# Pair 1 made as eight block products, its banks and its statistics order changed, in a graph-convolution kernel

## What is computed

```
h = relu(layernorm(x))                       # over the 1024 nodes
sim = cosine similarity of the nodes' mean;  adj = sim + gumbel0 > 1 - sim + gumbel1
nmask = adj or adj.T or eye;  common = nmask @ nmask.T
W = adj * common * common / max(common);     Wn = dinv * W * dinv
out = x + einsum(Wn, einsum(h, weight)) + bias
```

## Time and profile before

| | us |
|---|---|
| median of 3 runs | 839.84 (839.77 to 840.04) |
| the profiled execution | 838.23 |
| its span, first to last instruction | 836.5 |
| PE busy | 808.0 (97%) |
| DVE, ACT, POOL busy | 579.1, 495.9, 301.3 |

### The profile page before, as it was taken

How to read it: one execution, slowest core, us unless ns; L and a number is a source line. 1 busy time by engine, 2 the same in 40 slices (tenths; PEclk the granted TensorE clock), 3 DMA queues, 4 the chain that set the end, 5 groups by cost and what they waited for, 6 DMA issues and landing times.

```text
span 836.5 us, 13491 instructions
## 1 busy us (share of the span) xinstructions
PE 808.0 (97%) x4718; PEld 425.0 (51%) x4718; DVE 579.1 (69%) x689; ACT 495.9 (59%) x515; POOL 301.3 (36%) x255
## 2 busy tenths in 40 slices
PE   4999999999799999999999999999999999999997
PEld 3445466754345554555455545554555455545553
DVE  7999998699866656665666566656665666566652
ACT  3888826598466656665666456646655666456631
POOL 4788710300333334333433343334333333333320
PEclk9999999999999999999999999999999999999999
DMA  8999923001932222322232222222222222233111
GB/s 342 409 409 346 421 110 128 25 1 50 344 109 101 101 101 101 100 100 100 100 100 100 100 100 100 100 100 100 100 100 100 100 100 103 102 121 101 51 51 75
DMA packets 30121, 113.14 MB, mean 135 GB/s; under 512 B 3472, under 2 KB 3600, under 8 KB 29072
## 3 DMA queue, kind: packets, MB, share of 16 engines
q1 hardware_dynamic: 30096, 112.80, 36.8%
HBM read 79.23 MB, written 33.55 MB: 135 GB/s over the span
## 4 chain that ended last, share of the span: by engine, by line
PE 81%; DVE 13%; issue 3%; DMA 1%; ACT 1%; POOL 0%; DVEq 0%; SPq 0%; POOLq 0%; ACTq 0%
PE ps L891 65%; PE ps L808 8%; DVE stats L1001 8%; PE ps L907 2%; PE ps L743 2%; PE ps L826 2%; DVE moments L1007 1%; DMA out_dram<-obuf 1%; DVE ybuf L1022 1%; DVE a L1181 1%; DVE obuf L1263 0%; DVE a L1112 0%; PE ps L761 0%; PE ps L754 0%; DVE hring L1029 0%
## 5 line engine op out<-in xcount | busy, mean ns | idle before, releaser
L891 PE MATMUL ps<-a,ybuf 128*128 128x512 f16 x2604 | 571.0, 379 | 6.5 <-DVE ybuf L1105 3.4
L891 PEld LDWEIGHTS ps<-a,ybuf 128*128 128x128 f16 x2604 | 252.3, 98 | 302.7 <-DVE ybuf L1105 3.6
L1105 DVE TENSOR_TENSOR ybuf<-zbuf,ybuf 128x1024 f16<-128x1024 f32 x124 | 164.9, 1330 | 154.2 <-ACT ybuf L514 154.2
L389 POOL TENSOR_TENSOR zbuf<-zbuf 128x512 f32<-128x512 f32 x31 | 39.4, 1271 | 434.7 <-ACT zbuf L495 434.7
L514 ACT ACTIVATE ybuf<-zbuf 128x1024 f16<-128x1024 f32 x124 | 117.8, 950 | 109.6 <-POOL zbuf L394 93.9
L529 ACT ACTIVATE obuf<-ps,bias_sb,w_out 128x512 f32<-128x512 f32 x62 | 47.9, 772 | 122.8 <-PE ps L891 117.2
L1094 DVE TENSOR_TENSOR hring<-hring 128x1024 f16<-128x1024 f32 x53 | 71.1, 1342 | 56.2 <-ACT hring L473 56.1
L1263 DVE TENSOR_TENSOR obuf<-obuf,xring 128x1024 f32<-128x1024 f32 x64 | 80.4, 1258 | 2.7
L808 PEld LDWEIGHTS ps<-w,hring 128*128 128x128 f16 x1272 | 75.4, 98 | 12.4 <-issue 0.4
L808 PE MATMUL ps<-w,hring 128*128 128x128 f16 x1272 | 79.7, 219 | 0.3 <-DVE k L1138 0.3
L495 ACT ACTIVATE zbuf<-ps 128x1024 f32<-128x1024 f32 x55 | 56.3, 1024 | 33.3 <-PE ps L808 20.7
(11 more groups left out here) (140 smaller groups left out, 646.7 us busy)
## 6 DMA issues: line engine op xcount, KB each, us to landing
xring<-in_x_dram SPq DMA_DIRECT2D x96, 512.0 KB, 4.8
out_dram<-obuf SPq DMA_DIRECT2D x64, 512.0 KB, 2.9
ybuf<-in_x_dram SPq DMA_DIRECT2D x28, 512.0 KB, 7.6
a<-in_L_gnn_gumbel_dram SPq DMA_DIRECT2D x7, 1024.0 KB, 15.4
obuf<-in_x_dram SPq DMA_DIRECT2D x11, 512.0 KB, 5.9
obuf<-in_L_gnn_gumbel_dram SPq DMA_DIRECT2D x1, 1024.0 KB, 23.4
w<-in_adj_dram SPq DMA_DIRECT2D x1, 64.0 KB, 1.8
bias_sb<-in_L_gnn_bias_dram SPq DMA_DIRECT2D x1, 0.5 KB, 2.1
```

The costliest lines, as they stand in the source:

```text
L891: mm = nc.tensor.matmul(bank[q % 2], y16[:, q % 2, yk, u, c * P:(c + 1) * P], a16[:, ak, mat, c, :], start=(start and c == yk == ak == 0), ...
L1105: nc.vector.tensor_tensor(y16[:, q % 2, 1, a:a + n, :], z[:, a + 1:a + 1 + n, :], y16[:, q % 2, 0, a:a + n, :], ALU.subtract).then_inc(s_y, 1)
```

## The change

Pair 1 is made as eight block products too, in banks of its own (`SECOND_OUT`: ps_a[0], ps_b[0], ps_b[1], ps_d[1]); ACT writes its four blocks out (`second_out`), and DVE's `upper` and `lower` and POOL's `z_sums` of pair 1 are gone. Mats 3 to 6 are first read in pair 2. In DVE's code `low(6,5)` stands behind the two `add_x` of pair 0, and `low(7,6)` behind `y_low(0,2,2)`. At the start, DVE takes the statistics of batches 0 and 1 ahead of the weight's chain, `w16` is made by POOL, and the bias is loaded behind `x[0]` and `x[1]`.

```diff
+        SECOND_OUT = ((0, HI, ps_a[0]), (1, HI, ps_b[0]), (0, LO, ps_b[1]), (1, LO, ps_d[1]))
...
             sp.dma_start(w[:], adj).then_inc(s_consts, 16)
-            sp.dma_start(bias_sb[:], bias_col).then_inc(s_consts, 16)
-            for j in range(BODY1):
+            sp.dma_start(x1[0], x[0]).then_inc(s_x1[0], 16)
+            sp.dma_start(x1[1], x[1]).then_inc(s_x1[1], 16)
+            sp.dma_start(bias_sb[:], bias_col).then_inc(s_bias, 16)
+            for j in range(2, BODY1):
...
             norms(0, 0)
+            pool.wait_ge(s_wchain, 5)
+            nc.gpsimd.tensor_copy(w16[:, 0, :], w_inv[:]).then_inc(s_w16, 1)
+            pool.wait_ge(s_w16, 1)
+            nc.gpsimd.tensor_tensor(w16[:, 1, :], w_inv[:], w16[:, 0, :], ALU.subtract).then_inc(s_w16, 1)
...
-            pool.sem_inc(s_zs, 4)
-            z_sums(1)
+            pool.sem_inc(s_zs, 8)
...
             z_of(0, 1, 0)
-            y_high(0, 1, 0)
+            y_high_first(1, 0)
+            y_high_first(1, 1)
             copied(2)
             z_of(0, 1, 1)
-            y_high(0, 1, 1)
+            y_high_first(1, 2)
             copied(3)
             relu_first(4)
             copied(4)
-            y_high(0, 1, 2)
+            y_high_first(1, 3)
             copied(5)
-            y_high(0, 1, 3)
...
+            def second_out(n):
+                b, m, bank = SECOND_OUT[n]
+                act.wait_ge(s_mm, 14 + 7 + 2 * n + 1)
+                act.wait_ge(s_hhi, 3 + b)
+                nc.scalar.activation(o[1][b][:, m], bank, ACT.Identity, bias=bias_sb[:, 0:1],
+                                     scale=w_out[:, 0:1]).then_inc(s_first, 1)
...
             def second_pair():
...
+                pe.wait_ge(s_y, 12)
+                for n, (b, m, bank) in enumerate(SECOND_OUT):
+                    if n < 2:
+                        pe.wait_ge(s_first, n + 1)
+                    for k, mat in enumerate((0, 1) if m is LO else (A12, 2)):
+                        u = ((0, 3), (1, 2))[k][b]
+                        for c in range(HC):
+                            for yk, ak in ((0, 0), (0, 1), (1, 0)):
+                                mm = nc.tensor.matmul(bank, y16[:, 1, yk, u, c * P:(c + 1) * P], a16[:, ak, mat, c, :],
+                                                      start=(k == c == yk == ak == 0),
+                                                      stop=(k == 1 and c == HC - 1 and yk == 1), skip_group_check=True)
...
             low_part(3, 2, rows_lo, 1, 0)
-            y_low(0, 1, 3)
             low_part(3, 2, rows_lo, 1, 1)
...
-            upper0(0, 1)
-            upper1(0, 1)
             y_low(0, 2, 0)
             y_low(0, 2, 1)
             add_x(0, 0, 0)
             add_x(0, 0, 1)
+            low(6, 5, rows_hi[:, :, HI])
             h_low(0, 3, 1)
             y_low(0, 2, 2)
-            lower0(0, 1)
+            low(7, 6, spare)
+            y_low(0, 2, 3)
             add_x(0, 1, 0)
-            y_low(0, 2, 3)
-            lower1(0, 1)
             add_x(0, 1, 1)
```

More of the change, by code:

```diff
@@ L495, in z_of, with y_high_first @@
                 nc.scalar.activation(dst, src, ACT.Copy, scale=Y_SCALE / W_SCALE).then_inc(s_z, 1)
-            def y_high_first(u):
-                act.wait_ge(s_z, 2 if u >= 2 else 1)
-                nc.scalar.activation(y16[:, 0, 0, u, :], z[:, (u + 1) % 4, :], ACT.Copy).then_inc(s_yhi, 1)
+            def y_high_first(q, u):
+                act.wait_ge(s_z, 2 * q + (2 if u >= 2 else 1))
+                nc.scalar.activation(y16[:, q, 0, u, :], z[:, (u + 1) % 4, :], ACT.Copy).then_inc(s_yhi, 1)
             def y_high(i, q, g):
@@ L524, in partial @@
                     act.wait_ge(s_c, 4 * r + 6)
-                made = (1, 3, 4) if isinstance(r, int) and r == 1 else (1, 2, 3)
-                act.wait_ge(s_mm, 14 + 7 * r + made[k])
+                act.wait_ge(s_mm, 14 + 7 * r + k + 1)
                 dst = (o[q % 2][0][:, 0:H], p5[:], o[q % 2][0][:, H:N])[k]
@@ L622, in _ @@
             act.wait_ge(s_wout, 1)
+            act.wait_ge(s_bias, 16)
             act.wait_ge(s_fh, 3)
@@ L632, in _ @@
             high(4, rows_hi[:, :, LO])
[L633 to L637, removed]
+            z_of(0, 2, 0)
+            z_of(0, 2, 1)
+            y_high(0, 2, 0)
+            y_high(0, 2, 1)
+            second_out(0)
+            relu2(0, 3, 1)
             act.wait_ge(s_t, 3)
             high(5, rows_hi[:, :, HI])
[L640 to L647, removed]
+            second_out(1)
             y_high(0, 2, 2)
             y_high(0, 2, 3)
+            act.wait_ge(s_t, 4)
+            act.wait_ge(s_mm, 14 + 7 + 2)
+            high(6, spare)
+            second_out(2)
+            second_out(3)
             for q in range(2, PAIRS):
@@ L1143, in _ @@
             mask(1)
-            y_low(0, 1, 0)
+            y_low_first(1, 0)
+            y_low_first(1, 1)
             mask(2)
             mask(3)
-            y_low(0, 1, 1)
+            y_low_first(1, 2)
             mask(4)
-            y_low(0, 1, 2)
+            y_low_first(1, 3)
             mask(5)
@@ L1231, in _ @@
                                     ALU.subtract).then_inc(s_t, 1)
+            low(4, 3, spare)
+            low(5, 4, rows_hi[:, :, LO])
             dve.wait_ge(s_t, 2)
@@ L1234, in _ @@
             nc.vector.tensor_tensor(spare, rows_lo[:, :, LO], rows_hi[:, :, LO], ALU.subtract).then_inc(s_t, 1)
-            low(6, 5, rows_hi[:, :, HI])
-            low(7, 6, spare)
             def upper0(i, q):
                 r, ob = PAIRS * i + q, o[q % 2][0]
-                dve.wait_ge(s_mm, 14 + 7 * r + (5 if isinstance(r, int) and r == 1 else 4))
+                dve.wait_ge(s_mm, 14 + 7 * r + 4)
                 dve.wait_ge(s_v, 3 * r + 3)
```

102 lines of the change are left out of this document (47 added, 55 removed).

## The result

| | before | after |
| --- | --- | --- |
| median of 5 runs, us | 839.84 (838.80 to 840.04) | 843.35 (841.85 to 844.29) |
| after over before | | 1.0045, interval 1.0033 to 1.0057 |
| profiled execution / its span, us | 838.23 / 836.5 | 843.42 / 841.7 |
| granted clock, mean of the span | 0.998 (1.00 in every stretch of the earlier trace rows) | 0.993 |

The change costs 3.5 us by the medians and 3.8 by the recorded ratio, whose interval reaches from 2.8 to 4.8 us. The 842.6 us of the forecast are 0.75 too few, and the time lies within its range.

A forecast was written before the change was run, and what follows sets the result against it. The prediction took PE (busy 97%) as the bound, with gains possible only upstream and in the hand-over to pair 2. A late store, +3.5, less 0.75 upstream, gave +2.75 on 839.84: 842.6 us, range 838.3 to 844.9.

The forecast's parts named there:

- Upstream: Ahead of pair 1's products: 0.4 us from the new start and 0.35 from a narrower `y_low` in the counts, 0.75 gained.
- PE's own work: Pairs 1 and 2: pair 1 ends at 214.3, PE reaches mat 4's product at 220.9 instead of 225.40, 4.5 us gained if unobstructed.
- Step 1: DVE's T4, the instruction ahead of the loads of `x[0..3]`, still ends at 205.1; POOL takes back about 1.2 us.
- Step 2: DVE behind T4: 6.3 us of work plus 3.5 of turns with POOL's z sums, so `low(6,5)` ends at 214.9.
- Rival B: POOL does not hold DVE up; `low(6,5)` ends at 212.6 and the time is 839.4 to 841.1 us; chance 0.14.
- Step 3: SP's queue: batch 1's store stands behind the loads of `x[4..7]` and lands at 228.0, between 227.0 and 228.8.
- the low bound: Batch 1's store counted as seventh in SP's queue, one landing per 1.39 us: lands at 227.0.
- The forecast's own range: Whole kernel: 840.7 us (store at 227.0, all upstream gain) to 844.1 (229.2, little of it), holding chance 0.58.
- Rival A: Stores don't queue behind loads: batch 1's store lands 3.1 to 5.4 us after issue, time 836.0 to 838.3; chance 0.17.
- rival D: The stores are no limit at all, for instance because the landing comes early: 834.6 us; chance 0.03.
- Step 4: PE's product on mat 4 in pair 2 begins at 228.9 against 225.40, +3.5 us, after idling 8 us.
- the sum: Whole kernel: +3.5 us at PE's product less 0.75 upstream, +2.75 us.

The follow-up runs named there:

- experiment 4: The kernel before with only the edits of the start (early statistics, later bias load, `w16` by POOL): 838.01 us, ratio 0.9991.
- Experiment 2: The changed kernel with SP issuing the stores and reloads of batches 0 and 1 ahead of the loads of `x[4..7]`: 833.23 us, ratio 0.993.
- experiment 5: The changed kernel with POOL's z sums of pair 2 held back until `low(6,5)` is done: 840.92 us, ratio 1.0026.
- experiment 1: The changed kernel with `low(6,5)` moved back right behind T4, ahead of the `y_low` and `add_x` steps: 837.97 us, ratio 0.9985.
- Experiment 3: The changed kernel with 24 small products of zeros in PE's idle time before the third product of pair 2: 841.12 us, ratio 1.0031.
- experiment 8: The kernel before, old store order, with 10 small products of zeros in PE's 3.4 us wait before product 3 of pair 2: 838.99 us, ratio 1.001.
- experiment 6: The kernel before with the stores and reloads of batches 0 and 1 ahead of the loads of `x[4..7]`: 838.51 us, ratio 0.9999.
- experiment 7: The changed kernel with the four loads of `x[4..7]` issued on ACT's DMA queue instead of SP's: 842.12 us, ratio 1.0037.
- experiment 9: The kernel before with the stores of batches 0 and 1 ahead of the loads, plus 10 small products of zeros: 837.58 us, ratio 0.9987.

## Why the forecast held, point by point

**Upstream, 0.75 forecast, 0.76 found.** The second pair of batches and the counts in the timeline of the changed kernel:

```profile
5.01 2.72 DVE L1001 BATCH_NORM_STATS2 stats<-xring 128x6 f32<-128x512 f32 x4 [1.88 <-DMA xring<-in_x_dram]
...
9.60 2.50 DVE L1001 BATCH_NORM_STATS2 stats<-xring 128x6 f32<-128x512 f32 x4
...
158.05 0.38 ACT L559 ACTIVATE a<-ps 128x256 f16<-128x256 f32 x1 [1.02 <-PE ps L851]
158.54 1.23 DVE L1129 SCALAR_TENSOR_TENSOR a<-ps,xring 128x1024 f16<-128x1024 f32 x1
159.82 0.62 PE L842 MATMUL ps<-xring 128*128 128x128 f16 x8
172.14 20.88 PE L923 MATMUL ps<-a,ybuf 128*128 128x512 f16 x96 [0.19 <-DVE a L1193]
```

PE's product behind the same `mask` in the kernel before:

```profile
160.58 0.62 PE L826 MATMUL ps<-xring 128*128 128x128 f16 x8 [0.44 <-DVE a L1112]
```

The statistics start at 5.01 (5.0 forecast) and the second pair at 9.60 (9.5). The copy of count 5 comes 0.42 us sooner than before, and the next `mask` waits for the end of that copy and no more for a long `y_low`. Behind that `mask` PE is 0.76 us ahead (159.82 against 160.58), and still is at the first product of pair 1, 172.14 in place of 172.90. So the shares are in the trace: 0.42 from upstream and 0.34 from the narrow `y_low` (0.4 and 0.35 forecast). The first is less simple than I made it: the statistics end 0.84 us sooner (96.03 against 96.87), half of that is lost again by 109 us for a reason that I can't name, and in the profile of experiment 4, with the same start, only 0.1 us was left at the first product.

**PE's own work, 4.5 forecast.** No wait in pair 1, and it ended at 213.7 against 214.3 - 0.75 = 213.55. Experiment 2 shows that the 4.5 were there to be had: 5.4 us in all.

**Step 1, T4 at 205.1.** Less 0.75 that is 204.35, and it ended at 204.23. POOL took back 1.09 us in T4 itself, where 1.2 was forecast.

**Step 2, `low(6,5)` at 214.9.** Less 0.75: 214.15; it ended at 213.66. From T4's end it took 9.4 us where 9.8 was forecast (6.3 of work, 3.5 of turns). The turns behind T4 measured 3.2: `y_low` 3.97 us where it took 1.82 in experiment 5, the two `add_x` 3.42 where they take 2.35 alone, so about 1.1 for each z sum and not 1.2. Experiment 5 takes the turns away and has 211.40. Rival B is out by it. The rule that the prediction took from the GPSIMD Engine Reference of the Trainium skill, § 8. Key points, has the trace on its side: T4 at 3.37 against 2.28 us.

**Step 3, the store at 228.0.** Less 0.75: 227.25; it landed at 227.62, 10.63 us behind its issue. Counted from the end of `low(6,5)` the forecast had 13.1 us and the trace has 14.0, so the queue was 0.9 us worse than forecast, and step 2, 0.5 us too late, hid half of that. The count by places (1.39 us each), the low bound, gives 225.8 from 213.69, 1.8 us too soon; the store of before, eleventh from 205.2, would by it have been due at 222.9 and landed at 224.49, 1.6 later, and in experiment 1 it is 0.8 short. The choice near the middle came out; no mechanism had fixed it. The forecast's own range doesn't follow from its bounds either: 227.0 with 1.1 us of upstream gain gives 841.3 (840.7 is written) and 228.8 with 0.3 gives 843.8 (844.1). The measured median lies in both.

Rival A (3.1 to 5.4 us) fell by the landing at 227.62, and rival D with it. Experiment 2 shows that the place behind the loads is the cause, by turning the order round. The sentence that the prediction gave rival A from DMA: Bandwidth & Descriptors of the Trainium skill, § Queues, rings and completion order (a later descriptor may end sooner) left no sign at this store.

**Step 4, PE's product at 228.9.** Less 0.75: 228.15, measured 228.52, with a wait of 8.27 us for 8 forecast. ACT's wait was 13.1 us where I said some 11. ACT got there sooner than I thought. Behind it DVE waited 9.0 us for ACT's next `y_high`, but PE never came to wait for that.

**What the sum left out: the clock.** The sum ended at PE's product, and took it to run as before, which put the clock at nothing without a reason. It took 4.78 us, +2.02, because PE had been idle for 8.27 us and came back at the lower clock. Experiment 3 has the product back at 2.76 us by nothing but idle matmuls. TensorE: Matmul & The Clock Gate of the Trainium skill, § HAM oscillation, tells of this very pattern, matmuls that start slow behind a wait for a DMA; the trace agrees, and I did not weigh it. In the frame of the profiles the forecast of +2.75 met +5.2: 0.4 from the product's place and 2.0 from the clock. The wait and its cause were forecast right, and the size only because the next point covered for the clock.

**Why the median came out near all the same: luck, in good part.** The forecast was added to 839.84, the median of the kernel before that was known then. Its 71 executions beside the experiments have a median of 838.56 and lie in three groups: 9 from 836.7 to 837.6, 41 from 838.1 to 839.1 and 21 from 839.35 to 841.0. So the profiled execution, 838.23, was a typical one, and the three executions behind 839.84 were all of the upper group (of the five in the result's table, four). From 838.56 the forecast would have been 841.3, 2.0 us under the 843.35 that were measured, which is the size of the missing clock term; a base that was 1.3 us too high made up for most of it. That the change really costs nearer to 4.8 us (843.35 against 838.56) than 3.5 is likely but not shown, since it was not run beside those 71; 4.8 is the upper end of its recorded interval.

What makes the groups is known in part. The landing of batch 1's store differs by 1.4 us between two profiles (experiment 8), and the profiles of the experiments show falls of the clock in three places ahead of pair 2's third product or at it: behind the 3.4 us wait of the hand-over (experiments 4 and 6), near 23 us (experiments 2, 3 and 7) and near 112 us, as in this piece of experiment 2's stretches:

```profile
112.00:114.00 2.00, 2.00 (x12) 2.00 (x10) 0.35 (x1) 2.00 (x3) 1.21 (x2) 0.50 0.00 0
```

That profile's first product of pair 1 is at 173.87, 1.7 us later than in the changed kernel, with the same code up to there; 0.4 of it was there when the statistics ended (96.47 against 96.03), and the other 1.3 came behind it, with this fall. Which of these an untraced execution holds is not known.

**Where the gain went.** The eight block products are worth 4.5 us at PE, and the SP order alone is worth nothing (experiment 6). Together they give -5.4, apart +3.5 and 0 (medians). The gain was made and given back whole to the store of batch 1, which `low(6,5)`, moved behind `y_low` and `add_x`, pushed behind four loads that nobody was waiting for.

## What to carry to other kernels

When an edit moves the step that releases a group of loads, count the whole queue behind it from the first issue on, reloads and earlier stores too; where the DMA engines are full, put the transfer that an engine waits for ahead of those that nobody needs yet, before thinking of a second queue. A wait in front of matmuls can have a second price behind it, the lower clock (2.0 us here behind 8.3 us), and belongs in the sum as a term of its own. When an edit takes one wait away and the time stays, look for a second one of like size behind it (experiments 6, 8 and 9). And look whether the base of a forecast is typical: here the median of the first few executions was 1.3 us above that of 71, while the profiled one was close to it.

## What the runs showed of the hardware

- The same wait of 3.4 us in front of PE's product sometimes lowers its clock (experiments 4 and 6: 24 matmuls in 7.04 us; experiment 1: 12 in 4.45) and sometimes not (before: clock 1.00 at 222 to 224 us). Behind the 8.27 us wait it did in the changed kernel's profile (12 in 4.78 in place of 2.76).
- DVE and POOL pay for each other by the instruction: a DVE step of 2048 columns went from 2.28 to 3.37 us beside one z sum of 512 columns, which itself went from 1.27 to 3.24. The shorter the DVE step beside it, the less POOL paid (1.72 to 2.25 beside 1024 columns). Each of the four z sums cost DVE about 1.1 us.
- With the DMA engines full (a share of 1.00 from 216.5 to 226.8 us) a store issued from another queue than the four loads landed after 10.3 us; issued ahead of the loads it landed after 6.3, at a share of 0.99.
- The same store, issued at the same moment behind the same eight loads, let ACT go on at 224.57 us in one execution and at 223.17 in another.
